# Self attention's softmax denominators from ScalarE's accumulator in place of products with ones

## What is computed

```python
q, k, v = (proj(Wq), proj(Wk), proj(Wv))                 # (B, H, T, hd)
q = q * cos + _rotate_half(q) * sin
k = k * cos + _rotate_half(k) * sin
att = jnp.einsum('bhqd,bhkd->bhqk', q, k) / math.sqrt(hd)
att = jax.nn.softmax(att + mask, axis=-1)                # mask: -inf above the diagonal
out = jnp.einsum('bhqk,bhkd->bhqd', att, v)
return out.transpose(0, 2, 1, 3).reshape(B, T, D) @ Wo.T
```

## Time and profile before

| | |
|---|---|
| median of 3 runs | 1554.73 us (1553.87 to 1555.04) |
| the profiled execution | 1557.65 us, span 1555.9 us |
| PE busy | 1388.5 us, 89% of the span |
| PEld busy | 1139.0 us, 73% |
| DVE busy | 1015.6 us, 65% |
| ACT busy | 645.2 us, 41% |
| POOL busy | 334.8 us, 22% |
| TensorE clock, mean granted | 0.940 of full speed |

### The profile page before, as it was taken

One profiled execution on the slowest core, in us unless ns is written; L12 is line 12 of the kernel. 1 busy time (PEld: TensorE's weight loads), 2 busy tenths in 40 slices (PEclk: granted clock), 3 DMA queues, 4 the chain that ended last, 5 costly groups with the idle time before them and its releaser, 6 DMA issues. The chain is left out here.

```text
span 1555.9 us, 24568 instructions
## 1 busy us (share of the span) xinstructions
PE 1388.5 (89%) x8837; PEld 1139.0 (73%) x8837; DVE 1015.6 (65%) x1701; ACT 645.2 (41%) x1033; POOL 334.8 (22%) x491
## 2 busy tenths in 40 slices
PE   5999999999998679999999964699999999998990
PEld 5657666675665368888888854699999999997770
DVE  6767575577667275564654269677777777774777
ACT  3443244234243242423333142566565665663222
POOL 0242133123122210010100000322222222222562
PEclk9999999999998779999999985799999999998995
DMA  4200000000000131222220040677788777884563
GB/s 176 109 1 28 1 1 28 1 1 1 1 1 1 49 123 61 83 88 82 88 83 24 1 150 1 252 288 270 283 281 287 284 281 280 280 283 150 168 185 140
DMA packets 62024, 190.34 MB, mean 122 GB/s; under 512 B 7160, under 2 KB 7164, under 8 KB 61184
## 3 DMA queue, kind: packets, MB, share of 16 engines
q1 hardware_dynamic: 49312, 147.93, 26.5%
q0 software_dynamic: 12640, 41.43, 8.8%
HBM read 156.30 MB, written 33.03 MB: 122 GB/s over the span
## 5 line engine op out<-in xcount | busy, mean ns | idle before, releaser
L1527 DVE TENSOR_TENSOR e_w_sp<-e_w_raw,e_w_sp 128x1024 fp32r<-128x1024 f32 x141 | 168.6, 1221 | 17.9 <-ACT e_w_sp L1485 11.6
L438 PE MATMUL proj_ps<-wqkv,x_sp 128*128 128x384 f32 x768 | 170.9, 355 | 10.5 <-DVE wqkv L304 10.5
L1471 POOL DMA_INDIRECT e_x_g<-x_rows,e_index x94 | 101.3, 1078 | 321.7 <-DVE e_index L1538 307.1
L984 PE MATMUL c_score_ps<-ct,x_t 128*128 128x402 f32 x768 | 159.0, 359 | 0.0
L1485 ACT ACTIVATE e_w_sp<-e_w_raw 128x1024 fp32r<-128x1024 f32 x141 | 145.3, 1058 | 14.5 <-DMA e_w_raw<-w_experts 14.3
L1003 PE MATMUL c_out_ps<-cr,weigh_t 128*128 128x512 f32 (+1 forms) x624 | 147.3, 394 | 1.4 <-DVE weigh_t L843 1.4
L984 PEld LDWEIGHTS c_score_ps<-ct,x_t 128*128 128x128 f32 x768 | 140.6, 193 | 7.1 <-issue 5.3
L1586 PEld LDWEIGHTS e_gate_ps<-e_x_t,e_w_sp 128*128 128x128 f32 x1128 | 139.5, 190 | 5.9 <-DVE e_x_t L1548 1.8
L1586 PE MATMUL e_up_ps<-e_x_t,e_w_sp 128*128 128x256 f32 x1128 | 143.3, 283 | 0.0
L1586 PE MATMUL e_gate_ps<-e_x_t,e_w_sp 128*128 128x256 f32 x1128 | 141.0, 281 | 1.4 <-DVE e_x_t L1548 1.4
L438 PEld LDWEIGHTS proj_ps<-wqkv,x_sp 128*128 128x128 f32 x768 | 131.3, 194 | 11.1 <-issue 10.8
(11 more groups left out here) (205 smaller groups left out, 2231.8 us busy)
## 6 DMA issues: line engine op xcount, KB each, us to landing
e_w_raw<-w_experts SPq DMA_DIRECT2D x141, 512.0 KB, 5.6
y_rows<-e_y SPq DMA_DIRECT2D x47, 512.0 KB, 3.1
raw<-ctxT SPq DMA_DIRECT2D x16, 800.5 KB, 4.3
raw<-ctx_rows SPq DMA_DIRECT2D x16, 768.0 KB, 4.9
rows<-x_rows SPq DMA_DIRECT2D x1, 4096.0 KB, 12.2
x_rows<-rows SPq DMA_DIRECT2D x4, 1024.0 KB, 5.9
out<-rows SPq DMA_DIRECT2D x4, 1024.0 KB, 5.2
rows<-wqkvT SPq DMA_DIRECT2D x4, 768.0 KB, 7.3
```

What stands on the lines that cost most here:

```text
L438: mm = nc.tensor.matmul(proj_ps[:, tt, 0:GW], x_sp[:, xs, c, tt * P:(tt + 1) * P], wqkv[:, ws, c, hg * GW:(hg + 1) * GW], start=(c == 0 an ...
L984: mm = nc.tensor.matmul(score_ps[:, f, 0:MQ], x1_t[:, xs, c, qt * P:(qt + 1) * P], ct[:, cs, c, f * MQ:(f + 1) * MQ], start=False, stop=(c ...
L1471: nc.gpsimd.indirect_dma_start(x_g[:, par, half, :], None, x2_rows, bass.IndirectOffsetOnAxis(ap=index[:, par, half:half + 1], axis=0)).th ...
L1527: nc.vector.tensor_tensor(w_sp[:, par, part, 1, :], w_raw[:, par, part, :], w_sp[:, par, part, 0, :].bitcast(F32), ALU.subtract).then_inc( ...
```

## The change

The score tiles go round three banks (`row_place`: the two of `score_ps`, then `den_ps`). Behind each maximum, which DVE now writes negated, ACT takes the exponential of the tile in place in PSUM, with the maximum as bias, and its accumulator output gives the sum of the row (`row_sum`). PE writes a bank again when that exponential is done. ACT's other work of the score half goes between these exponentials. DVE inverts the 16 columns of sums at once; PE turns them into `den_ps`, repeated over 32 rows a head, with 16 products with the identity (`turn_inverse`, behind the fourth score tile of the second half); DVE keeps them in `o_f` (`keep_inverse`, behind `rotate`). `weight_sums` and `invert_sums` are gone. The projection's 48 products are dealt out anew: 36 in the score half, 4 before the maxima's transposes, 4 behind, 4 between the first two pairs of the second half. The next group's turns are issued before the last `values`. The factor 1/sqrt(hd) moves into the tables of cosines and sines. The diff, indented less, without a few renamed lines:

```diff
 scored_t, exped, summed = sem("scored_t"), sem("exped"), sem("summed")
-den_inv, o_scaled, o_hi, o_lo = sem("den_inv"), sem("o_scaled"), sem("o_hi"), sem("o_lo")
+row_exped, inverted, inv_turned, inv_kept = sem("row_exped"), sem("inverted"), sem("inv_turned"), sem("inv_kept")
+o_scaled, o_hi, o_lo = sem("o_scaled"), sem("o_hi"), sem("o_lo")
 out_proj, res_added = sem("out_proj"), sem("res_added")
 NG = B * HG
+NS = TT * GH
+def row_place(n):
+return score_ps[:, n % 3, :] if n % 3 < 2 else den_ps[:, :]
 assert HG == TT
...
-        act.wait_ge(scored_t, g * GH * TT)
+        act.wait_ge(scored_t, g * NS)
         for h in range(GH):
                                  ACT.Copy).then_inc(q_stacked, 1)
-        if hg == HG - 1 and not last:
-            hi_x(b + 1, 2)
-            hi_x(b + 1, 3)
-        if not first:
-            hi_out(g - 1, (hg - 1) % HG)
-        if hg == HG - 2 and b < B - 1:
-            hi_x(b + 1, 0)
-            hi_x(b + 1, 1)
+        for n in range(NS):
+            qt, h = n // GH, n % GH
+            w = (qt + 1) * P
+            act.wait_ge(maxed, g * NS + n + 1)
+            if n == 0:
+                act.wait_ge(inverted, g)
+            nc.scalar.activation(row_place(n)[:, 0:w], row_place(n)[:, 0:w], ACT.Exp,
+                                 bias=neg_row_max[:, qt, h:h + 1], accum_out=row_sum[:, qt, h:h + 1]
+                                 ).then_inc(row_exped, 1)
+            if n in (1, 3) and hg == HG - 1 and not last:
+                hi_x(b + 1, 2 + n // 2)
+            if n == 6 and not first:
+                hi_out(g - 1, (hg - 1) % HG)
+            if n == 7 and g == 0:
+                hi_wo()
+            if n in (9, 11) and hg == HG - 2 and b < B - 1:
+                hi_x(b + 1, n // 2 - 4)
...
                 n = kc * GH + h
-                act.wait_ge(scored_t, g * GH * TT + n + 1)
+                act.wait_ge(scored_t, g * NS + n + 1)
                 nc.scalar.activation(p_t[:, h, p_at[kc]:p_at[kc] + w],
-                                     score_ps[:, n % 2, kc * P:T], ACT.Exp,
-                                     scale=float(HD) ** -0.5).then_inc(exped, 1)
+                                     score_ps[:, n % 2, kc * P:T], ACT.Exp).then_inc(exped, 1)
                 if n == 2 * GH + 1 and not last:
                     hi_q(g + 1)
-        if g == 0:
-            hi_wo()
...
-    sums_t = qk_sin[:, 0, :, :].rearrange("p t (n j) -> p (t n) j", j=HD)
-    inv_t = qk_sin[:, 1, 0, 0:T // HD]
-    def invert_sums(g, part):
-        if part == 0:
-            dve.wait_ge(summed, g + 1)
-            nc.vector.transpose(sums_t, den_ps[:, :].rearrange("p (n j) -> p n j", j=HD)
-                                ).then_inc(den_inv, 1)
-        elif part == 1:
-            dve.wait_ge(den_inv, g * 3 + 1)
-            nc.vector.reciprocal(inv_t, sums_t[:, :, 0]).then_inc(den_inv, 1)
-        elif part == 2:
-            dve.wait_ge(o_lo, g)
-            dve.wait_ge(den_inv, g * 3 + 2)
-            nc.vector.transpose(o_f[:, :].rearrange("p (n j) -> p n j", j=HD),
-                                inv_t.unsqueeze(2).broadcast_to([P, T // HD, HD])).then_inc(den_inv, 1)
+    def keep_inverse(g):
+        dve.wait_ge(inv_turned, g + 1)
+        dve.wait_ge(o_lo, g)
+        nc.vector.tensor_copy(o_f[:, :], den_ps[:, :]).then_inc(inv_kept, 1)
-        dve.wait_ge(den_inv, g * 3 + 3)
+        dve.wait_ge(summed, g + 1)
+        dve.wait_ge(inv_kept, g + 1)
         nc.vector.tensor_tensor(o_f[:, :], o_ps[:, :], o_f[:, :], ALU.mult).then_inc(o_scaled, 1)
...
                 n = qt * GH + h
-                dve.wait_ge(scored, g * GH * TT + n + 1)
+                dve.wait_ge(scored, g * NS + n + 1)
                 if n == 0:
                     dve.wait_ge(max_lo, g)
-                nc.vector.tensor_reduce(row_max[:, qt, h:h + 1], score_ps[:, n % 2, 0:(qt + 1) * P],
-                                        AX, ALU.max).then_inc(maxed, 1)
-                if n % 2 == 1 and n < 2 * GH and not first:
-                    if n // 2 < 3:
-                        invert_sums(g - 1, n // 2)
-                    elif n // 2 == 3:
-                        finish_out(g - 1)
-        dve.wait_ge(maxed, g * GH * TT + GH * TT)
+                    dve.wait_ge(row_exped, g * NS)
+                nc.vector.tensor_reduce(neg_row_max[:, qt, h:h + 1], row_place(n)[:, 0:(qt + 1) * P],
+                                        AX, ALU.max, negate=True).then_inc(maxed, 1)
+                if n == 3 and not first:
+                    finish_out(g - 1)
+        dve.wait_ge(maxed, g * NS + NS)
         dve.wait_ge(max_turned, g)
-        nc.vector.tensor_scalar(neg_max[:, :, :, 0], row_max[:, :, :], -1.0, None,
-                                ALU.mult).then_inc(max_hi, 1)
+        nc.vector.tensor_copy(neg_max[:, :, :, 0], neg_row_max[:, :, :]).then_inc(max_hi, 1)
         dve.wait_ge(max_hi, g + 1)
-        nc.vector.scalar_tensor_tensor(neg_max[:, :, :, 1], row_max[:, :, :], -1.0,
-                                       neg_max[:, :, :, 0].bitcast(F32), ALU.mult, ALU.subtract
-                                       ).then_inc(max_lo, 1)
+        nc.vector.tensor_tensor(neg_max[:, :, :, 1], neg_row_max[:, :, :],
+                                neg_max[:, :, :, 0].bitcast(F32), ALU.subtract).then_inc(max_lo, 1)
         if hg == 0 and not first:
...
                                   ).then_inc(max_stacked_v, 1)
+        dve.wait_ge(row_exped, g * NS + NS)
+        dve.wait_ge(inv_turned, g)
+        nc.vector.reciprocal(row_sum[:, :, :], row_sum[:, :, :]).then_inc(inverted, 1)
         if not last:
             rotate(g + 1)
+        keep_inverse(g)
         if g == 0:
     groups(group)
-    for part in range(3):
-        invert_sums(NG - 1, part)
     finish_out(NG - 1)
...
                 pe.wait_ge(res_added, b * TT + tt - 1)
+            if tt == 0 and b == B - 1:
+                pe.wait_ge(inv_kept, NG)
+            if tt == 1 and b < B - 1:
+                pe.wait_ge(row_exped, (b + 1) * HG * NS + NS)
             for c in range(HG):
...
                 pe.wait_ge(k_stacked, g * GH + h + 1)
-            if n >= 2:
-                pe.wait_ge(maxed, g * GH * TT + n - 1)
+            if n >= 3:
+                pe.wait_ge(row_exped, g * NS + n - 2)
+            elif n == 2:
+                pe.wait_ge(inv_kept, g)
             else:
-                pe.wait_ge(exped, g * GH * TT)
+                pe.wait_ge(exped, g * NS)
             wide = max(w, 2 * P)
-            nc.tensor.matmul(score_ps[:, n % 2, 0:wide], q_st[0:3 * HD, h, qt * P:w],
+            place = row_place(n)
+            nc.tensor.matmul(place[:, 0:wide], q_st[0:3 * HD, h, qt * P:w],
                              k_st[0:3 * HD, h, 0:wide], start=True, stop=False)
-            nc.tensor.matmul(score_ps[:, n % 2, w - P:w], ident_b[:, :], mask_qk[:, :],
+            nc.tensor.matmul(place[:, w - P:w], ident_b[:, :], mask_qk[:, :],
                              start=False, stop=True).then_inc(scored, 1)
...
         for h in range(GH):
-            nc.tensor.matmul(o_ps[h * HD:(h + 1) * HD, kc * P:T], v[:, hg % 2, kc, h * HD:(h + 1) * HD],
-                             p_t[:, h, p_at[kc]:p_at[kc] + T - kc * P],
-                             start=(kc == 0), stop=(kc == TT - 1))
-    def weight_sums(g, kc):
-        for h in range(GH):
-            mm = nc.tensor.matmul(den_ps[h * HD:(h + 1) * HD, kc * P:T], ones[:, :],
+            mm = nc.tensor.matmul(o_ps[h * HD:(h + 1) * HD, kc * P:T],
+                                  v[:, hg % 2, kc, h * HD:(h + 1) * HD],
                                   p_t[:, h, p_at[kc]:p_at[kc] + T - kc * P],
-    def group(b, hg, first, last):
-        g = b * HG + hg
+    def turn_inverse(g):
+        pe.wait_ge(inverted, g + 1)
+        pe.wait_ge(max_stacked_a, (g + 1) * (GH // 2))
+        pe.wait_ge(max_stacked_v, (g + 1) * (GH // 2))
+        for qt in range(TT):
+            for h in range(GH):
+                mm = nc.tensor.matmul(den_ps[h * HD:(h + 1) * HD, qt * P:(qt + 1) * P],
+                                      row_sum[:, qt, h:h + 1].broadcast_to([P, HD]), ident_f[:, :],
+                                      start=True, stop=True)
+        mm.then_inc(inv_turned, 1)
+    def turn_heads(g):
...
-        STEP = 5
+    STEPS = (5, 5, 4, 4, 4, 5, 4, 5)
+    BEFORE_TURN, BEHIND_TURN, BETWEEN_SCORES = 4, 4, 4
+    assert sum(STEPS) + BEFORE_TURN + BEHIND_TURN + BETWEEN_SCORES == len(products)
+    def group(b, hg, first, last):
+        g = b * HG + hg
+        done = 0
+        def project_next(n):
+            nonlocal done
+            if not last:
+                project(g + 1, (hg + 1) % HG, done, done + n)
+            done += n
         for n in range(2 * TT):
             scores(g, n // 2, n % 2)
-            if not last:
-                project(g + 1, (hg + 1) % HG, n * STEP, (n + 1) * STEP)
+            project_next(STEPS[n])
         if hg == 0 and not first:
```

(28 more changed lines are left out.)

## The result

| kernel | median of 4, us | range | profiled execution | its span |
|---|---|---|---|---|
| before | 1554.88 | 1553.87 to 1555.07 | 1557.65 | 1555.9 |
| after | 1542.51 | 1541.52 to 1543.42 | 1543.42 | 1541.7 |

The ratio is 0.9922, 95% interval 0.9904 to 0.9939: faster by 12.4 us, where 22.9 had been forecast. Run again later it gave 1539.28 (0.9913, 0.9898 to 0.9929).

What follows compares the result with a forecast made beforehand. PE's own instructions bound the score half, waits for exponentials and POOL the second half. Terms 12.8, 4.3, 3.1 and 3.2 sum to 23.4 us, taking the 1554.73 median to 1531.3, rounded up to 1532; range 1522 to 1551.

Steps and rivals of the forecast that it cites:

- 11 plain intervals: Groups without output projection: 1.6 us gained less 0.4 in the score half, 1.2 each, less 4 x 0.1; 12.8 in all.
- 3 with `project_out`: Groups with the output projection: 1.6 us gained less 0.15, as products cover the last exponential; 4.3 in all.
- first group: Start of the stage, with `hi_wo` moved into the score half: 3.4 + 1.2 - 1.5, a gain of 3.1 us.
- last group: Stage's end: inversion out of the way 1.85, last sums 0.4, other sums and inversion pieces about 1.0; 3.2 us gained.
- Second half: From the maxima's transposes to the turns: 11.1 us against 12.95, 1.85 less, `turn_inverse` taking 0.96 within PE's waits.
- Turns to score: Last `values` now stands between the turns and the next group's scores: 0.25 us more.
- Score half: From first score to maxima's transposes: 12.8 us against 12.41, 0.4 more, from waits for row exponentials to free banks.
- Clock: Four falls to half clock among the groups, counted before the change, were taken as unchanged; one cost 1.55 us.
- C: Rival: the clock stays up because the second half's thin start is filled; four falls go, 6 us, time 1526; chance 0.10.
- D: Rival: the clock falls in every group because the later second half is thin; 12 more falls, 1551 us; chance 0.10.
- B: Rival: ACT paces the score half, each row exponential holding it 0.19 us longer; 11 us more, 1543; chance 0.17.
- E: Rival: column groups of `turn_inverse` do not run side by side; it takes 3.8 us, time 1578; chance 0.08.

Runs made afterwards that it cites:

- e6: The changed kernel with the 16 products of `turn_inverse` issued twice over; 1561.31 us, ratio 1.0046 to before.
- e7: The changed kernel with rotate's two additions on VectorE cut to one column, output not the reference's; 1541.39 us, ratio 0.9914.
- e3: The changed kernel with each row exponential replaced by one of a single column in SBUF, output not the reference's; 1525.56 us, ratio 0.9809.
- e4: The changed kernel with the maxima's transposes waiting for the last row exponential but one, and the next score tile for the last; 1536.21 us, ratio 0.9872.
- e10: e9 with the rounding of wo cut in quarters, two in group 0 and two in group 1; 1529.32 us, ratio 0.9834.
- e11: The changed kernel unedited, run once more beside the versions built on it; 1539.28 us.
- e2: The changed kernel with the next group's turns put behind the last `values` again; 1560.61 us, ratio 1.0041.
- e9: e8 with the 16 products of `turn_inverse` issued as four sets of four between score tiles of the second half; 1530.66 us, ratio 0.9842.
- e8: e4 with score tiles issued singly between 2 or 3 products each, in place of pairs between 4 or 5; 1536.96 us.
- e5: The changed kernel with the four products between the second half's first score pairs moved ahead of the maxima's transposes; 1553.87 us, ratio 0.9999.

## Why the prediction was right in sign and half in size

The span fell by 14.2 us. Read from both traces, against the prediction's terms:

| term | forecast | measured |
|---|---|---|
| 11 plain intervals | 12.8 | 8.0 and 1.55 of clock |
| 3 with `project_out` | 4.3 | 2.8 and 2.2 of clock |
| first group | 3.1 | -0.6 |
| last group | 3.2 | 3.05 |
| behind the stage | 0 | -2.8 |

- **Second half: the failed step.** "The first `values` has to wait for POOL until 4.6 anyway, so behind it the next pair goes at 5.6 as before." It went at 6.02 (201.14 - 195.12). The inverse itself was nearly right (1.08 against 0.96), but it starts at 3.48, not 3.3, and between it and `values` stand tiles 4 and 5, 0.54 of PE time that the walk left out: 3.48 + 1.01 + 0.54 = 5.03. From there to the turns it is 5.42, where the forecast had 5.5. PE's waits at this place of before, which were to hide the inverse, sum to 1.07 - 0.54 = 0.53 only (its second pair ends at 229.89, the first `values` starts at 230.96, tiles 4 and 5 stand between). Shown by e6 and e7. Price 0.34 a group.
- **Turns to score: under-priced.** 0.45 in place of 0.25. The last `values` costs 0.36 (209.16 to 209.52), and the turns 0.09 more. I had priced the set by the start of the next one in a run of equal ones (0.24); ahead of a score tile it took 0.36.
- **Score half: right.** 12.78 against 12.8; the row exponential took 0.660 at 512 columns where 0.685 was summed; e3 puts the ring and the last exponential together at 1.05, e4 the last exponential alone at 0.22 to 0.26.
- **With `project_out`: over-priced.** An undisturbed interval went from 39.32 to 38.40, 0.92 each instead of 1.45; it shares the two faults above.
- **First group: wrong sign.** `hi_wo` stops the ring at 37.24 in after, and PE waits 1.24 for it until 39.76; that was foreseen. Not foreseen: its low part, 2.28 us of VectorE at 54.64, stretches the two masks beside it to 2.38, and PE waits 1.79 for them until 57.36. So most of the 3.4 that had been counted as gone came back in a new form (the interval is 29.89, 2.7 over a plain one). e10 gets 2.0 back. Of the 2.0 by which the first maxima are late, 0.9 is not the edit's: run again the same kernel had them at 43.56.
- **Clock.** "I take the number as unchanged": in the profiled executions the half-clock stretches in the middle of the stage went from four (from 60.87, 173.51, 258.84 and 299.80) to two (59.31 and 417.71; the row from 418.00 below shows the second), in e11 to two, in e2 to five. But before's profiled execution has a mean granted clock of 0.940, and 31 of the 38 others of before whose clock is on record have 0.944 to 0.946; the ten of the changed kernel have 0.942 to 0.946. So what the table calls clock was gained against one unusual execution, the medians show no gain from it, and C is not borne out. D is refuted: the 32 transposes behind the thinned second half ran at 1.00 (second row), and 15 groups of them brought two falls. That is the reading of the trace that the prediction set against the Trainium skill ("TensorE: Matmul & The Clock Gate", Part 4).
```profile
418.00:421.00 3.00, 3.00 (x25) 2.19 (x25) 0.34 (x1) 1.36 (x4) 2.10 (x5) 0.50 0.00 0
...
206.56:209.20 2.64, 2.64 (x36) 2.48 (x38) 1.78 (x3) 2.12 (x6) 0.92 (x4) 1.00 0.00 0
```
- **Behind the stage.** Of what the stage gained 2.2 us went in cross attention and 0.6 behind it. By the granted clock, full speed came back 20.9 us behind the stage's end before (559.2 - 538.3) and 22.7 after (544.0 - 521.3). From cross attention's first transposes to the table load it took 348.1 in before, 350.5 in after, 350.6 in e11, 349.6 in e9, 348.5 in e10 and 347.4 in e8, with no edit there. In the 40 us from those transposes on, before and e10 were at half clock for 16.3, after and e11 for 18, e9 for 18.9, e8 for 11.9. So the loss goes, in the main, with when the clock changes, which the forecast could not see; why it changes when it does stays open.
- **B** (ACT paces) fell near the measured time, for none of its reasons: exponentials were 0.67 apart where they followed closely, and the score half was not longer than forecast. **E** is refuted by 1.08, and by e6.

Part of the profiled gain was not the change's either: before's profiled execution lay 2.8 above its median, after's 0.9.

That the stated range of 1522 to 1551 held the time is in part luck. The measured 1542.5 lies outside the forecast's own 1526 to 1540, and the upper part of the range stood there for B and for D's edge, neither of which happened. The chances given for faster (0.55, 0.17, 0.10 and half of 0.10) add up to 0.87, not 0.85.

## What to carry to other kernels

When cheap work is put into a queue "under" a wait, walk everything that stands in the same queue between it and the waiting instruction; the slack is what is left behind all of that, not the wait's own end. Two edits that meet in one queue must be priced together: alone one gave 0.46 us a group and the other cost 0.28 (2.2 gained and 6.8 lost on the medians), together they gave 0.66 (12.4). And before a slow neighbour is called the cause, make it fast: the mask stretched from 0.29 to 0.64 looked like the answer and was worth nothing here, while the same contention cost 0.48 a group once e5 had moved it.

## What the hardware showed

- A VectorE operation that reads SBUF alone, with two inputs (L335, L346) or one (L341), and a POOL mask hold each other, and the one that starts first goes undisturbed. In after all 46 masks that start inside such an operation end 0.15 behind its end, the fourth of a group after 0.64 in place of 0.29; all 30 that start up to 0.15 before one keep their 0.29, and the operation takes 0.75 to 0.78 in place of 0.69. The fourth mask is back at 0.29 when the operation is cut short (e7). The six masks of e5 that took 3.27 were three of 0.77 to 0.85 beside L335, L341 and L346, and three of 0.29 beside VectorE's reads of PSUM.
- ScalarE's exponential with bias, from PSUM to PSUM in place, took 0.335, 0.444, 0.55 and 0.66 us at 128, 256, 384 and 512 columns. Its accumulator read shows 0.197, but the next instruction starts 0.67 behind the start of one of 512 columns.
- Sixteen float32 products of 32 stationary columns, read from one column by broadcast, and 128 moving ones took 1.08 us in one run, 32 of them 1.95, but four alone 0.42.
